# Long exponentials in place in PSUM, two projections over two steps, low query weights on GpSimd, another order on ScalarE and VectorE

## What is computed

```python
q = _rms_norm(x @ wq_a.T, q_norm_w) @ wq_b.T            # 32 heads, 128 plain + 64 rotary
kv_c, k_pe = kv[..., :KV_LORA], kv[..., KV_LORA:]       # 64 latent, 64 rotary
kv_up = _rms_norm(kv_c, kv_norm_w) @ wkv_b.T
k_nope, v = kv_up[..., :QK_NOPE], kv_up[..., QK_NOPE:]
scores = (einsum('bshd,bthd->bhst', q_nope, k_nope) + einsum('bshd,btd->bhst', q_pe, k_pe)) * scale
probs = softmax(where(causal, scores, min))
out = einsum('bhst,bthd->bshd', probs, v) @ wo.T
```

## Time and profile before

| | us |
|---|---|
| median of three executions | 1525.0 |
| lowest, highest | 1512.6, 1527.8 |
| the profiled execution | 1517.9 |
| its span | 1516.1 |

### The profile page before, as it was taken

The page is one execution under the profiler, slowest core; times in us unless marked ns, Lnnn a source line. Parts: engine busy times, 40 slices in busy tenths (PEclk is TensorE's granted clock), DMA queues, the critical chain, the costliest instruction groups (busy, mean ns, idle before and its releaser), DMA issues. The chain is left out here.

```text
span 1516.1 us, 32860 instructions
## 1 busy us (share of the span) xinstructions
PE 1320.1 (87%) x13058; PEld 905.5 (60%) x13058; DVE 1102.5 (73%) x1664; ACT 955.1 (63%) x1690; POOL 776.8 (51%) x759
## 2 busy tenths in 40 slices
PE   4899995988989998999988899999889898479997
PEld 4787773666666666666666666666666666334443
DVE  3755454788888888888888888888888889542321
ACT  3644433777777777777777777777777778641120
POOL 0222011777677767767766776776776674000110
PEclk8999997999999999999999999999999999889999
DMA  4011004788899888799898888979888897799995
GB/s 158 29 56 57 28 21 138 136 161 145 155 173 171 163 147 157 157 162 173 153 161 152 155 159 163 167 159 172 141 161 154 157 168 139 178 182 228 247 244 131
DMA packets 573641, 225.85 MB, mean 149 GB/s; under 512 B 509232, under 2 KB 552880, under 8 KB 572848
## 3 DMA queue, kind: packets, MB, share of 16 engines
q1 hardware_dynamic: 562992, 199.09, 68.3%
q0 software_dynamic: 10496, 24.66, 7.2%
HBM read 55.91 MB, written 25.17 MB: 53 GB/s over the span
## 5 line engine op out<-in xcount | busy, mean ns | idle before, releaser
L737 ACT ACTIVATE prob_long_sb<-score_long,shift_sb 128x1024 f32<-128x1024 f32 (+3 forms) x256 | 245.0, 957 | 250.0 <-DVE shift_sb L853 249.8
L859 DVE TENSOR_TENSOR prob_hl_sb<-prob_long_sb,prob_hl_sb 128x1024 f16<-128x1024 f32 (+3 forms) x256 | 358.0, 1398 | 0.0
L853 DVE TENSOR_REDUCE shift_sb<-score_long 128x1 f32<-128x1024 f32 (+3 forms) x256 | 259.4, 1013 | 68.1 <-PE score_long L649 67.6
L828 POOL TENSOR_TENSOR ql_sb<-qf_sb,qh_sb 128x512 f16<-128x512 f32 x124 | 144.8, 1169 | 233.9 <-ACT qh_sb L757 233.9
L745 ACT ACTIVATE prob_hl_sb<-prob_long_sb 128x1024 f16<-128x1024 f32 (+3 forms) x256 | 232.5, 908 | 0.0
L646 PE MATMUL score_long<-key_hi,qh_sb 128*128 128x512 f16 (+3 forms) x512 | 176.3, 344 | 10.0 <-DVE ql_sb L914 9.1
L659 PE MATMUL flip<-ident_sb,prob_short_sb 128*128 128x128 f32 x640 | 117.4, 281 | 73.9 <-DVE ptl_short_sb L865 73.7
L845 POOL TENSOR_TENSOR qf_sb<-qf_sb,rot_sb 64x512 f32<-64x512 f32 x124 | 174.1, 1404 | 9.5
L821 POOL DMA_DIRECT2D rot_sb<-qf_sb x248 | 124.8, 508 | 104.6 <-DVE ql_sb L914 61.3
L680 PE MATMUL acc<-ch,prob_t_sb 128*128 128x65 f16 x1664 | 177.5, 192 | 0.0
L678 PE MATMUL acc<-ch,prob_t_sb 128*128 128x65 f16 x1664 | 177.2, 194 | 0.3 <-DMA prob_t_sb<-prob_hl_sb 0.3
(11 more groups left out here) (180 smaller groups left out, 3396.8 us busy)
## 6 DMA issues: line engine op xcount, KB each, us to landing
o<-o_sb SPq DMA_DIRECT2D x32, 512.0 KB, 4.5
o_nat_sb<-o SPq DMA_DIRECT2D x32, 512.0 KB, 6.8
rot_sb<-qf_sb POOLq DMA_DIRECT2D x248, 64.0 KB, 3.5
wqk_sb<-wqk SPq DMA_DIRECT2D x32, 320.0 KB, 4.4
wo_sb<-wo SPq DMA_DIRECT2D x16, 512.0 KB, 4.2
x_sb<-x SPq DMA_DIRECT2D x4, 1024.0 KB, 4.8
y<-y_sb SPq DMA_DIRECT2D x16, 256.0 KB, 2.0
wq_f_sb<-wqp SPq DMA_DIRECT2D x32, 128.0 KB, 4.5
```

The lines of the kernel that those rows point to most:

```text
L737: nc.scalar.activation(prob[kind][:, s % 2, 0:width(s, kind)], score_of(s, kind), ACT.Exp, bias=shift[:, s % (2 * WIN), kind:kind + 1], sc ...
L853: nc.vector.tensor_reduce(shift[:, s % (2 * WIN), kind:kind + 1], score_of(s, kind), AX.X, ALU.min).then_inc(shift_ready[kind], 1)
L859: nc.vector.tensor_tensor(prob_hl[:, s % NHL, n:2 * n], prob[LONG][:, s % 2, 0:n], prob_hl[:, s % NHL, 0:n], ALU.subtract).then_inc(lo_rea ...
```

## The change

- The long exponential is written over its own scores in PSUM. `prob_long` goes, `high_long` and `low_long` read PSUM, and PE's long scores of step s wait for `low_long` of step s-2 instead of the exponential.
- Two of the four projections are split: three terms at the end of one step and two at the end of the next (steps 3 and 4 for place 0, 5 and 6 for place 1). Place 1 is therefore complete, and taken by ACT, in step 6 instead of 4.
- `weights_low` of all pairs but the first two moves from DVE to POOL, into the second half of each pair, behind `query_low`. It has a semaphore of its own, `wl_later`, for which PE waits ahead of place 0's first terms, and SP ahead of the next load of weights, now in step 4.
- ACT does `high_short` of step s-1 ahead of the long exponential of step s. DVE does `low_long` between the two minima, `low_short` behind them, and `outputs` last.

```diff
--- before.py
+++ after.py
@@ -483,7 +483,7 @@
         rot = sb("rot", [P, 2, 512], F32)
         qf = sb("qf", [P, 2, 2, 512], F32)
 
-        prob = [sb("prob_short", [P, 2, 512], F32), sb("prob_long", [P, 2, S], F32)]
+        prob = sb("prob_short", [P, 2, 512], F32)
         prob_hl = sb("prob_hl", [P, NHL, 2 * S], F16)
         prob_t = sb("prob_t", [P, NPT, 2 * ST, P], F16)
         pth, ptl = sb("pth_short", [P, NPS, 512], F16), sb("ptl_short", [P, NPS, 512], F16)
@@ -494,7 +494,7 @@
         NCONST, const_in, cast_ready = 3, sem("const_in"), sem("cast_ready")
         w_in, wo_in = [sem("wq_in0"), sem("wq_in1")], sem("wo_in")
         absorb_mm, lat_ready, wh_ready, wl_ready = (sem(n) for n in ("absorb_mm", "wlat_ready", "wh_ready", "wl_ready"))
-        vo_mm, wo_ready = sem("vo_mm"), sem("wo_ready")
+        vo_mm, wo_ready, wl_later = sem("vo_mm"), sem("wo_ready"), sem("wl_later")
         proj_mm, proj_out, rot_mul, rot_add, qh_ready, ql_ready = (
             sem(n) for n in ("proj_mm", "proj_out", "rot_mul", "rot_add", "qh_ready", "ql_ready"))
         first_in, rot_in = [sem("first_in0"), sem("first_in1")], [sem("rot_in0"), sem("rot_in1")]
@@ -521,8 +521,9 @@
             return (tile(s, kind) + 1) * P
 
 
-        PIECE = {0: (1, 3), 3: (2, 0), 4: (2, 1), 7: (2, 2)}
-        PIECE_FIRST = {0: (1, 2), 1: (1, 3), 4: (2, 0), 5: (2, 1), 7: (2, 2)}
+        PIECE = {0: (1, 3), 4: (2, 0), 6: (2, 1), 7: (2, 2)}
+        PIECE_FIRST = {0: (1, 2), 1: (1, 3), 4: (2, 0), 6: (2, 1), 7: (2, 2)}
+        BEGUN, TERMS = {4: 3, 6: 3}, 5
         HIGH = {1: (0,), 2: (1,), 5: (2,), 6: (3,)}
         HIGH_FIRST = {3: (0, 1), 6: (2, 3)}
         absorb_at, high_weights_at = lambda s: s % WIN == (2 if s < WIN else 1), lambda s: s % WIN == (3 if s < WIN else 2)
@@ -590,8 +591,8 @@
                 if u == 2 and w % 2 == 1 and w + 1 < WINS:
                     sp.wait_ge(vo_mm, w + 1)
                     load_wo((w + 1) // 2)
-                if u == 3 and w + 4 < WINS:
-                    sp.wait_ge(wl_ready, w + 3)
+                if u == 4 and w + 4 < WINS:
+                    sp.wait_ge(wl_later, w + 1)
                     load_w(w + 4)
                 if u == LAG and w >= 1:
                     store(w - 1)
@@ -620,7 +621,7 @@
                                           wo[:, h, w % 2 * H // 2:(w % 2 + 1) * H // 2], start=True, stop=True)
                 mm.then_inc(vo_mm, 1)
 
-            def project(n, out=proj[:]):
+            def project(n, out=proj[:], first=0, end=TERMS):
 
 
                 p, c, h = n // 4, n // 2 % 2, n % 2
@@ -628,9 +629,10 @@
                 cols = slice(h * P, (h + 1) * P)
                 at = slice(b * S + c * 512, b * S + (c + 1) * 512)
                 terms = ((wh, 0, lat_hi, 0), (wh, 0, lat_lo, 0), (wl, 0, lat_hi, 0), (wh, 1, lat_hi, 1), (wl, 1, lat_hi, 1))
-                for i, (w, t, q, kind) in enumerate(terms):
-                    mm = nc.tensor.matmul(out, w[j][:, t, cols], q[:, kind, at], start=(i == 0), stop=(i == 4))
-                mm.then_inc(proj_mm, 1)
+                for i, (w, t, q, kind) in list(enumerate(terms))[first:end]:
+                    mm = nc.tensor.matmul(out, w[j][:, t, cols], q[:, kind, at], start=(i == 0), stop=(i == TERMS - 1))
+                if end == TERMS:
+                    mm.then_inc(proj_mm, 1)
 
             def scores(s, kind):
 
@@ -656,7 +658,7 @@
                     pe.wait_ge(ptl_ready, s)
                 for j in range(tile(s, SHORT) + 1):
                     at = slice(j * P, (j + 1) * P)
-                    mm = nc.tensor.transpose(flip[:, at], prob[SHORT][:, s % 2, at], ident[:])
+                    mm = nc.tensor.transpose(flip[:, at], prob[:, s % 2, at], ident[:])
                 mm.then_inc(flip_mm, 1)
 
             def values(s):
@@ -698,7 +700,7 @@
                     if u == 0 and w >= 1:
                         pe.wait_ge(ql_ready, 4 * w)
                     if s >= 2:
-                        pe.wait_ge(exp_ready[LONG], s - 1)
+                        pe.wait_ge(lo_ready, s - 1)
                     scores(s, LONG)
                     if s >= 1:
                         pe.wait_ge(exp_ready[SHORT], s)
@@ -714,12 +716,18 @@
                     values(t)
                 if s < STEPS:
                     n = piece_at(s)
-                    if n is not None:
+                    if n is not None and u in BEGUN:
+                        project(n, first=BEGUN[u])
+                    elif n is not None:
+                        pe.wait_ge(proj_out, n)
+                        project(n)
+                    if u + 1 in BEGUN and piece_at(s + 1) is not None:
+                        n = piece_at(s + 1)
                         pe.wait_ge(proj_out, n)
                         if n % 4 == 0:
-                            pe.wait_ge(wl_ready, n // 4 + 1)
+                            pe.wait_ge(wl_later, n // 4 - 1)
                             pe.wait_ge(wo_ready, w + 1)
-                        project(n)
+                        project(n, end=BEGUN[u + 1])
                     if absorb_at(s):
                         pe.wait_ge(proj_out, min(4 * (w + 2), 4 * WINS))
                         if w >= WINS - 2:
@@ -732,9 +740,10 @@
         def _(act):
             def exp(s, kind):
                 act.wait_ge(shift_ready[kind], s + 1)
-                if s >= 2:
-                    act.wait_ge(lo_ready if kind == LONG else flip_mm, s - 1)
-                nc.scalar.activation(prob[kind][:, s % 2, 0:width(s, kind)], score_of(s, kind), ACT.Exp,
+                if kind == SHORT and s >= 2:
+                    act.wait_ge(flip_mm, s - 1)
+                out = score_of(s, LONG) if kind == LONG else prob[:, s % 2, 0:width(s, SHORT)]
+                nc.scalar.activation(out, score_of(s, kind), ACT.Exp,
                                      bias=shift[:, s % (2 * WIN), kind:kind + 1], scale=-1.0).then_inc(exp_ready[kind], 1)
 
             def high_long(s):
@@ -742,7 +751,7 @@
                     act.wait_ge(turn_in[(s - NHL) % NPT], turned(s - NHL))
                 act.wait_ge(exp_ready[LONG], s + 1)
                 n = width(s, LONG)
-                nc.scalar.activation(prob_hl[:, s % NHL, 0:n], prob[LONG][:, s % 2, 0:n], ACT.Copy).then_inc(hi_ready, 1)
+                nc.scalar.activation(prob_hl[:, s % NHL, 0:n], score_of(s, LONG), ACT.Copy).then_inc(hi_ready, 1)
 
             def high_short(s):
                 if s >= NPS:
@@ -783,10 +792,10 @@
             act.wait_ge(const_in, 16 * NCONST)
             for s in range(STEPS):
                 w, u = s // WIN, s % WIN
+                if s >= 1:
+                    high_short(s - 1)
                 exp(s, LONG)
                 exp(s, SHORT)
-                if s >= 1:
-                    high_short(s - 1)
                 high_long(s)
                 n = piece_at(s)
                 if n is not None:
@@ -828,6 +837,11 @@
                     nc.gpsimd.tensor_tensor(ql[:, 2 * (p % 2) + h, at], qf[:, c, h, :], qh[:, 2 * (p % 2) + h, at],
                                             ALU.subtract).then_inc(ql_ready, 1)
 
+            def weights_low(p):
+                pool.wait_ge(wh_ready, p + 1)
+                nc.gpsimd.tensor_tensor(wl[p % 2][:], wf[p % 2][:], wh[p % 2][:].bitcast(F32),
+                                        ALU.subtract).then_inc(wl_later, 1)
+
             for k in range(2, 2 * WINS):
 
                 c = k % 2
@@ -835,6 +849,8 @@
                 swap_halves(k)
                 if k > 2:
                     query_low(k - 1)
+                if c == 1 and k // 2 + 1 < WINS:
+                    weights_low(k // 2 + 1)
                 pool.wait_ge(rot_in[c], 64 * (k // 2))
                 nc.gpsimd.tensor_tensor(rot[:, c, :], rot[:, c, :], sinT[:, at], ALU.mult)
                 for h in range(2):
@@ -856,7 +872,7 @@
             def low_long(s):
                 dve.wait_ge(hi_ready, s + 1)
                 n = width(s, LONG)
-                nc.vector.tensor_tensor(prob_hl[:, s % NHL, n:2 * n], prob[LONG][:, s % 2, 0:n], prob_hl[:, s % NHL, 0:n],
+                nc.vector.tensor_tensor(prob_hl[:, s % NHL, n:2 * n], score_of(s, LONG), prob_hl[:, s % NHL, 0:n],
                                         ALU.subtract).then_inc(lo_ready, 1)
 
             def low_short(s):
@@ -918,15 +934,15 @@
                 w, u = s // WIN, s % WIN
                 if s < STEPS:
                     least(s, LONG)
+                if 1 <= s <= STEPS:
+                    low_long(s - 1)
+                if s < STEPS:
                     least(s, SHORT)
+                if 1 <= s <= STEPS:
+                    low_short(s - 1)
                 t = s - LAG
                 if t >= 0 and t % 2 == 1:
                     outputs(t)
-                if 1 <= s <= STEPS:
-                    low_long(s - 1)
-                    low_short(s - 1)
-                if s < STEPS and high_weights_at(s) and w + 2 < WINS:
```

(1 more changed line is left out.)

## The result

The changed kernel takes 1592.5 us in the median (1586.6 to 1594.7), the kernel before 1524.9 in the same comparison: a ratio of 1.045, 95% interval 1.040 to 1.051. It is slower by 68 us, where 20 were forecast, and lies above the range of 1518 to 1572. The sign, and the two places where PE waits, were as forecast; the size was not.

What follows compares the result with a forecast made beforehand. No engine is full; a closed chain sets the end, with DVE mostly late. Parts of 8.24, 8.27, 7.34 and 9.59 give a 33.36 us window against 32.94; with first and last windows +20 us, 1545 us, range 1518 to 1572.

Steps and rivals of the forecast that it cites:

- T0 to T2: From PE's long scores of step 0 to those of step 2: forecast 8.24 us for 8.68.
- T4 to T6: From PE's long scores of step 4 to those of step 6: DVE's loop sets it, 7.34 us for 8.08.
- The long rounding of 640 columns: On DVE, with one input in PSUM: forecast 0.81 us for 1.78, by the short rounding's slope.
- The new loop over the PSUM halves: PE's long scores wait for DVE's rounding of the long exponential: 3.62 us from T4 to T5, 3.72 for step 5.
- PE's wait behind POOL's low queries at step 0: Low queries stand behind the swap on POOL, so PE, and DVE behind it, stand some 2.2 us.
- the two POOL chains: From step 2 via low weights to PE's projection, 8.27 us; from step 6 via swap and low queries to T0, 9.59.
- ACT's half of the new orders: ACT's short rounding ahead of the long exponential: delays it by 0.07 us in steps 2 and 6.
- T2 to T4: From PE's long scores of step 2 to those of step 4: a draw, 8.27 us for 8.26.
- T6 to T0: From PE's long scores of step 6 to those of the next step 0: 9.59 us for 7.92.
- the 0.08 taken off for ACT's reads: In the window's sum, 0.04 us less twice for ACT reading PSUM: 33.44 becomes 33.36.
- The draw at the low weights: Step 2 to 4: the 2.1 us taken from DVE come back as PE's wait for POOL, 8.27 against 8.26.
- The rival that has POOL and DVE slow each other: Rounding of 640 stays 1.78 us, POOL's new instruction takes 2.1: +52, 1597 us; chance 0.06.

Runs made afterwards that it cites:

- projections back: The changed kernel with both projections whole again, in steps 3 and 4 as in the kernel before: 1520.1 us, ratio 0.999.
- PSUM and orders: The kernel before with the long exponential in PSUM and both new orders on ACT and DVE, projections and low weights unchanged: 1506.5 us, ratio 0.989.
- the split alone: The kernel before with the two projections spread over two steps each and nothing else: 1632.5 us, ratio 1.071.
- the low weights on DVE: The changed kernel with the low query weights back on DVE, at the end of its step 2: 1604.3 us, ratio 1.051.
- the low queries first: The changed kernel with POOL's two low queries ahead of the four swapping DMAs in the even half of a pair: 1610.9 us, ratio 1.059.

## Why the prediction was wrong in size

**The bound and the method held.** Reading the window as parts between the starts of PE's long scores gave T0 to T2 8.24 (measured 8.21) and T4 to T6 7.34 (7.26). The long rounding of 640 columns takes 0.81 us now, as taken from the short rounding's slope:

```profile
L875 DVE TENSOR_TENSOR prob_hl_sb<-score_long,prob_hl_sb 128x640 f16<-128x640 f32 x57 | 46.4, 814 | 0.0
```

It answers to the 1783 ns of the earlier trace rows; what POOL ran beside it no longer matters. POOL gains too: its multiplication with the sine takes 1279 ns in the mean of 57, where 1.25 was taken for an undisturbed one. The new loop over the PSUM halves is there at its forecast length, and PE's wait behind POOL's low queries at step 0 is in every window, 2.49 us for the forecast 2.2.

**The step that failed is the short exponential's place in the two POOL chains.** The prediction wrote that "ACT's starts are apart by 0.80, 0.47, 0.73" in both chains. The 0.80 came from a kernel in which the short minimum follows directly on the long one. The change puts DVE's long rounding of some 1 us between them. Of that edit the prediction priced only what it does to the loop over the PSUM halves, and took ACT's half of the new orders as 0.07. In steps 2 and 6 ACT's short exponential now starts 1.25 and 1.34 after the long one. In step 2 the long one is late as well, by 0.14: it starts 2.44 us after PE's start of the step and not 2.30, since ACT's short rounding, now ahead of it, stands there behind the copies of step 1; this is ACT's half of the orders, taken as 0.07. Together that is +0.56 in T2 to T4 and +0.51 in T6 to T0; the two other parts came out 0.11 shorter than their terms, and the 0.08 taken off for ACT's reads was not there on top. The window is 1.04 longer than forecast, 30 us in 29 windows. The run with the short minimum first in steps 2 and 6 takes 0.97 of this away (0.41 and 0.56 in the two parts) and leaves ACT's 0.14. That it lands at 1547 against the 1545 of the forecast is closer than the terms are: its first window and the one at the change of batch are longer than forecast, and beside the kernel before in its own comparison it is slower by 25 us, not 20.

**The second miss is the clock, which the sum did not have.** The prediction found a wait of over 2 us for PE in every window and charged its length alone. In six windows PE's next work was slower as well, some 11 us in all. With a wait of 1.7 instead of 2.5 us it was left in one window; in the kernels without that wait (projections back; PSUM and orders) there is no such window.

**The draw at the low weights was a draw for another reason.** The prediction set PE's wait for POOL against DVE's 2.1 us and called it even. The runs say that both sides were incomplete: put back on DVE in the changed kernel, the low weights delay the rounding that frees PSUM (the window +0.1); with the projections whole, POOL is the worse place for them (the window +0.35); and moved to POOL without the PSUM exponential, they are slowed to 1.98 us (+1.6 a window, the half clock in the projection included). The rival that has POOL and DVE slow each other does not hold in the changed kernel, and does in that one. Its time, 1597, is near the measured 1592.5 by coincidence: neither of its two terms is there: the rounding takes 0.81 us and POOL's low weights 1.26.

**The terms that were right.** The first window +7.5 for +6.5; the release to PE 0.06 to 0.11 for 0.10; POOL's four issues 2.01. The rule of the Trainium skill that was weighed (GPSIMD Engine Reference, "Engine selection": two-input work at about twice VectorE's time) would have given 1.44 us for the low weights on POOL; the trace gives 1.26, and the row decided rightly. The other rule of the Trainium skill (ScalarE: Activation LUTs, "Step-by-step: what each stage is for": writing to PSUM is faster) agrees with the trace in sign: the long exponential of 768 columns, the one in both chains, takes 886 ns into PSUM and took 906 into SBUF, 0.04 us of a window.

## What to carry to other kernels

When an instruction is moved in an engine's order, price it on both sides: what it delays, and what the one behind it released. A duration between two starts in the old trace is only valid as long as the order of the engine that releases the second is the same. In an in-order queue, look at what stands behind the instruction that now waits longer, and at when the DMA that it issues will land in the traffic of its new place. Buffers freed by a later reader turn that reader's engine into part of the producer's loop; such a change needs the reader's order to go with it, and each of the two alone can cost more than both together gain.

## What the runs showed of the hardware

- TensorE at half its clock for some 2.6 us after waits of 2.1 to 5.5 us (granted clock 0.50 from 711.30 to 713.90 us of the kernel after), but not after each: two waits of 2.49 and 2.48 us in the same execution ended one with it and one without. By the wait ahead of step 0: 1.7 us, no window in two kernels; 2.15 us, 16 windows (the split alone); 2.5 us, 5 windows in the changed kernel and 11 with the low weights on DVE.
- A swap of 64 KB lands in 2.1 us in the median in the kernel with the projections back, in 4.1 in the changed one, and 7.6 us after its last issue in the kernel with the low queries first, with other transfers beside it in each.
- Two-input instructions of POOL and DVE that both read SBUF twice stretch each other: 1.26 to 1.98 us for the same one on POOL, 0.72 to 1.23 on DVE. With one of DVE's inputs in PSUM neither is stretched.
- The stage `combine`, the same instructions in all kernels, took between 201.8 and 219.8 us in the fourteen profiled executions. This is as wide as the spread of a kernel's runs, and it is why a profile's own time should be compared by stage.
